# Weights of q and k loaded during the graph stage, and the last graph batch's tail spread over the engines

## The reference, cut to what matters

```python
# first layer: graph attention, two directions, 20 key rows, 16 heads
self_feat = concat([x, q_exp]) @ W_self.T + b_self
for d in range(2):
    w = softmax(where(mask, q @ k.T / sqrt(dh), NEG) + label_bias)
    output = output + (w @ kv) @ Wout[d] + bout[d]
x = x + relu(output)
# second layer
h = gamma * layernorm(x) + beta
q, k, v = split(h @ Wqkv.T + bqkv)                 # 16 heads of 32
att = softmax(q @ k.T) / sqrt(512)
h1 = (att @ v) @ Wp.T + bp + x
y = gamma * layernorm(h1) + beta + h1
```

## Time and profile before

| | |
|---|---|
| time, median of 3 runs | 1591.75 us (1589.45 to 1593.44) |
| the profiled execution | 1588.15 us, of which span 1586.4 |
| prologue | 0 to 116 us |
| graph stage | 116 to 652 us |
| attention stage | 652 us to the end |
| busy over the span | PE 87%, DVE 58%, POOL 57%, ACT 40% |
| mean granted TensorE clock | 0.927 of full speed |

### The profile page before, as it was taken

One profiled execution on the slowest core, in us unless ns is written; L12 is line 12 of the kernel. 1 busy time (PEld: TensorE's weight loads), 2 busy tenths in 40 slices (PEclk: granted clock), 3 DMA queues, 4 the chain that ended last, 5 costly groups with the idle time before them and its releaser, 6 DMA issues.

```text
span 1586.4 us, 19843 instructions
## 1 busy us (share of the span) xinstructions
PE 1376.4 (87%) x5988; PEld 873.2 (55%) x5988; DVE 923.2 (58%) x1494; ACT 631.1 (40%) x1090; POOL 899.5 (57%) x568
## 2 busy tenths in 40 slices
PE   6986998898898995279999999999999999999974
PEld 3644665665665663155565656555556555656532
DVE  2541665665664755136566757576667566666744
ACT  0231323324334232315454545545545445454551
POOL 1004434545545524316466958778769578687793
PEclk9997899999998987579999999999999999999977
DMA  9454213333323212724224425344344244253310
GB/s 297 177 174 129 83 65 132 136 113 135 125 106 153 86 60 106 265 73 109 73 61 127 114 61 147 94 107 108 87 127 111 62 127 111 70 143 89 104 46 27
DMA packets 107192, 179.41 MB, mean 113 GB/s; under 512 B 41312, under 2 KB 50848, under 8 KB 101840
## 3 DMA queue, kind: packets, MB, share of 16 engines
q1 hardware_dynamic: 94976, 143.92, 29.5%
q10 hardware_dynamic: 12112, 34.24, 7.2%
HBM read 81.06 MB, written 46.17 MB: 80 GB/s over the span
## 4 chain that ended last, share of the span: by engine, by line
PE 19%; POOL 17%; issue 8%; DVE 8%; ACT 3%; DMA 1%; SPq 1%; ACTq 1%; POOLq 0%; DVEq 0%
POOL acc L1022 7%; PE a_bank L1444 4%; PE a_bank L1407 4%; DVE rden L1295 4%; POOL acc L1017 3%; PE a_bank L1420 3%; PE a_bank L48 2%; PE a_bank L49 2%; PE a_bank L50 2%; DVE mx L1277 2%; PE a_bank L1455 2%; POOL h L1046 2%; POOL tn L1045 2%; ACT pt L1169 1%; DMA pt<-in_wp_t 1%
## 5 line engine op out<-in xcount | busy, mean ns | idle before, releaser
L1277 DVE TENSOR_REDUCE mx<-a_bank 128x1 f32<-128x512 f32 x512 | 341.9, 674 | 275.0 <-PE a_bank L1420 273.3
L1169 ACT ACTIVATE pt<-a_bank 128x512 f32<-128x512 f32 x512 | 301.9, 597 | 380.6 <-PE a_bank L1407 354.7
L1022 POOL TENSOR_TENSOR acc<-acc,pt 128x1024 f32<-128x1024 f32 x128 | 305.1, 2384 | 18.1 <-ACT pt L1169 9.9
L1407 PE MATMUL a_bank<-sq_stack,sk_stack 98*128 98x512 f32 x512 | 227.6, 447 | 31.1 <-ACT pt L1169 15.1
L1420 PE MATMUL a_bank<-sk_stack,sq_stack 96*128 96x512 f32 x512 | 220.0, 433 | 21.0 <-DVE mx L1277 19.7
L1017 POOL TENSOR_TENSOR acc<-pt 128x1024 f32<-128x1024 f32 x64 | 152.7, 2386 | 117.4 <-PE a_bank L1455 77.4
L1407 PEld LDWEIGHTS a_bank<-sq_stack,sk_stack 98*128 98x128 f32 x512 | 98.6, 193 | 158.3 <-issue 97.7
L774 PE MATMUL g_bank<-m,sf 128*128 128x320 f32 x512 | 161.9, 461 | 1.9 <-issue 1.9
L1420 PEld LDWEIGHTS a_bank<-sk_stack,sq_stack 96*128 96x128 f32 x512 | 99.9, 195 | 68.7 <-DVE mx L1277 54.6
L1295 DVE RECIPROCAL rden<-a_bank 128x128 f32<-128x128 f32 x128 | 120.1, 942 | 20.2 <-PE a_bank L1455 20.2
L48 PE MATMUL a_bank<-hh,wqkh 128*128 128x512 f32 x256 | 104.4, 408 | 27.5 <-DVE wqkl L1365 27.5
(11 more groups left out here) (164 smaller groups left out, 2540.6 us busy)
## 6 DMA issues: line engine op xcount, KB each, us to landing
sq_stack<-qh SPq DMA_DIRECT2D x256, 64.0 KB, 2.0
sk_stack<-kh SPq DMA_DIRECT2D x256, 64.0 KB, 2.3
m_rows<-mout SPq DMA_DIRECT2D x8, 1280.0 KB, 5.0
m<-m_rows SPq DMA_DIRECT2D x8, 1280.0 KB, 5.7
xraw<-in_x_t SPq DMA_DIRECT2D x8, 1024.0 KB, 7.5
xn<-in_x SPq DMA_DIRECT2D x8, 1024.0 KB, 6.8
h_rows<-xn ACTq DMA_DIRECT2D x8, 1024.0 KB, 3.9
t_rows<-houth SPq DMA_DIRECT2D x8, 1024.0 KB, 3.9
```

Of the source, the lines that this page charges most:

```text
L1022: nc.gpsimd.tensor_tensor(acc[:, two, :], acc[:, two, :], pt[:, step + 1, two, :], ALU.add).then_inc(s["sum_done"], 1)
L1169: nc.scalar.activation(pt[:, i, 2 * half + k, :], bank[:, k, :], ACT.Exp).then_inc(s["exp_done"], 1)
L1277: nc.vector.reduce_max(mx[:, half, k, n:n + 1], bank[:, 2 + e % 2, :], AX).then_inc(s["emax_done"], 1)
L1407: nc.tensor.matmul(bank[:, k, :], sk[0:3 * DH + 2, c % 2, j, i * P:(i + 1) * P], sq[0:3 * DH + 2, c % 2, j, :], start=True, stop=True).the ...
```

## The change

- The tile `v` and the four semaphores of the raw weights are made outside of the blocks, so that they exist through all of them. To make room, `vparts` of the prologue lies in the first half of `wself_raw`, and DVE waits for POOL's `w1l` before it writes there.
- SP loads the raw weights of q and k at the end of steps 1 and 2 of the graph stage into v[:, 0] and v[:, 1]. At the attention stage's start it loads v's and wp's only.
- The split into high and low parts is made by chunks of 512 columns, with a semaphore count for each. ACT's order is: q, k, qh of unit (0,0), v, kh, three values, wp. DVE's: q, k, ql, v, kl, ql and kl of unit (0,1). TensorE waits chunk by chunk.
- In the last graph batch DVE makes `hout` from PSUM, ACT rounds it into `houth`, POOL subtracts for chunks 0 and 2 and DVE for 1 and 3. DVE then adds bp to the four tiles of xn, behind everything else. ACT issues the h store after that.

```diff
--- before.py
+++ after.py
@@ -76,7 +76,7 @@
         mout = sb("mout", [P, 2, B, HK])
-        vparts = sb("vparts", [P, 2, 2, D], F32R)
+        vparts = wself_raw[:, 0:FC, :].rearrange("p (g k) o -> p g k o", g=2).bitcast(F32R)
         bank = ctx.enter_context(nc.psum_tensor("p_bank", [P, 8, 512], F32))
@@ -219,6 +219,8 @@
                     dve.wait_ge(s["v_ready"], n + 1)
+                    if n == 0:
+                        dve.wait_ge(s["w1_split"], 1)
                     if e == 1:
...
@@ -442,6 +444,9 @@
                     load_m(b + 1)
+                if isinstance(b, int) and b < 3:
+                    sp.dma_start(t["v"][:, b - 1], d["wqkv_t"][:, b - 1, :].rearrange("(c p) o -> p c o", p=P)
+                                 ).then_inc(t["w_in"][b - 1], 16)
@@ -537,9 +542,10 @@
             back(B - 1)
-            for i in range(NT):
-                add_bp(B - 1, i)
-            lo_rows(B - 1)
+            for f in (0, 2):
+                pool.wait_ge(s["lnt_done"], 4 * (B - 1) + f + 1)
+                nc.gpsimd.tensor_tensor(houtl[:, f, :], hout[:, f, :], houth[:, f, :].bitcast(F32),
+                                        ALU.subtract).then_inc(s["hl_done"], 1)
@@ -626,8 +632,10 @@
             normalise(B - 1)
+            act.wait_ge(s["t_stored"], 32 * (B - 1))
             for f in range(FC):
-                scale_ln(B - 1, f)
+                act.wait_ge(s["ho_done"], f + 1)
+                nc.scalar.activation(houth[:, f, :], hout[:, f, :], ACT.Copy).then_inc(s["lnt_done"], 1)
             store_h(B - 1)
@@ -734,6 +742,18 @@
             residual_ln(B - 1)
+            dve.wait_ge(s["gb_in"], 16 * 2 * FC)
+            dve.wait_ge(s["hl_done"], 4 * (B - 1))
+            for f in range(FC):
+                dve.wait_ge(s["lnt_ready"], 4 * (B - 1) + f + 1)
+                nc.vector.tensor_scalar(hout[:, f, :], bank[:, 2 + f, :], gcol[:, f, B - 1:B], bcol[:, f, B - 1:B],
+                                        ALU.mult, ALU.add).then_inc(s["ho_done"], 1)
+            for f in (1, 3):
+                dve.wait_ge(s["lnt_done"], 4 * (B - 1) + f + 1)
+                nc.vector.tensor_tensor(houtl[:, f, :], hout[:, f, :], houth[:, f, :].bitcast(F32),
+                                        ALU.subtract).then_inc(s["hl_done"], 1)
+            for i in range(NT):
+                nc.vector.tensor_tensor(xn[:, i, :], xn[:, i, :], bp[:, :], ALU.add).then_inc(s["hb_done"], 1)
@@ -865,7 +885,7 @@
         sq, sk = sb("sq_stack", [P, 2, HC, N], F32R), sb("sk_stack", [P, 2, HC, N], F32R)
-        v = sb("v", [P, 2, NT, D])
+        v = t["v"]
         pt = sb("pt", [P, NT, HC, N])
...
@@ -893,11 +913,11 @@
         STK = 16 * 6
-        w_in = tuple(s["w_in%d" % k] for k in range(4))
+        w_in = t["w_in"]
         t_in = (s["t_in0"], s["t_in1"])
...
-        raw = tuple(pt[:, k] for k in range(4))
+        raw = (v[:, 0], v[:, 1], pt[:, 0], pt[:, 1])
         hi_lo = ((t["wqkh"][:, :, 0:D], t["wqkl"][:, :, 0:D]), (t["wqkh"][:, :, D:2 * D], t["wqkl"][:, :, D:2 * D]),
@@ -989,7 +1009,7 @@
             sp.dma_start(bcol3[:, :, :], d["bqkc"]).then_inc(s["ld_c"], 16)
-            for k in range(4):
+            for k in (2, 3):
                 src = d["wqkv_t"][:, k, :] if k < 3 else d["wp_t"]
@@ -1006,6 +1026,13 @@
         def _(pool):
+            def split_lo():
+
+                for f in range(FC):
+                    pool.wait_ge(s["wp_hi"], f + 1)
+                    nc.gpsimd.tensor_tensor(hi_lo[3][1][:, f, :], raw[3][:, f, :], hi_lo[3][0][:, f, :].bitcast(F32),
+                                            ALU.subtract).then_inc(s["wp_lo"], 1)
+
             def key_sum(b, c, half, step):
@@ -1080,8 +1107,7 @@
             pool.wait_ge(s["set_up"], 3)
-            pool.wait_ge(s["w_hi"], 4)
-            nc.gpsimd.tensor_tensor(hi_lo[3][1], raw[3], hi_lo[3][0].bitcast(F32), ALU.subtract).then_inc(s["w_lo_pool"], 1)
+            split_lo()
             batches(pool, batch)
@@ -1097,6 +1123,13 @@
         def _(act):
+            def split_hi(k, chunks):
+
+                act.wait_ge(w_in[k], 16)
+                for f in chunks:
+                    nc.scalar.activation(hi_lo[k][0][:, f, :], raw[k][:, f, :], ACT.Copy
+                                         ).then_inc(s["w_hi"] if k < 3 else s["wp_hi"], 1)
+
             def load_t(b):
@@ -1239,13 +1272,14 @@
             act.wait_ge(s["ld_c"], 16)
-            for k in range(4):
-                act.wait_ge(w_in[k], 16)
-                nc.scalar.activation(hi_lo[k][0], raw[k], ACT.Copy).then_inc(s["w_hi"], 1)
+            split_hi(0, range(FC))
+            split_hi(1, range(FC))
             project(0, 0, 0)
+            split_hi(2, range(FC))
             project(0, 0, 1)
...
                 values(0, 0, i, src)
+            split_hi(3, range(FC))
             project(0, 1, 0)
@@ -1360,12 +1394,19 @@
             dve.wait_ge(s["bv_done"], 1)
-            for k in range(3):
-                dve.wait_ge(s["w_hi"], k + 1)
-                nc.vector.tensor_tensor(hi_lo[k][1], raw[k], hi_lo[k][0].bitcast(F32), ALU.subtract).then_inc(s["w_lo"], 1)
-            for c in range(2):
-                lo_part(0, c, 0)
-                lo_part(0, c, 1)
+            def split_lo(k):
+                for f in range(FC):
+                    dve.wait_ge(s["w_hi"], FC * k + f + 1)
+                    nc.vector.tensor_tensor(hi_lo[k][1][:, f, :], raw[k][:, f, :], hi_lo[k][0][:, f, :].bitcast(F32),
+                                            ALU.subtract).then_inc(s["w_lo"], 1)
+
+            split_lo(0)
+            split_lo(1)
+            lo_part(0, 0, 0)
+            split_lo(2)
+            lo_part(0, 0, 1)
+            lo_part(0, 1, 0)
+            lo_part(0, 1, 1)
             for slot in range(SLOTS):
@@ -1561,15 +1602,14 @@
-            pe.wait_ge(s["w_lo"], 1)
-            for f in range(FC):
-                project(0, 0, 0, f)
-            pe.wait_ge(s["w_lo"], 2)
-            for f in range(FC):
-                project(0, 0, 1, f)
-            pe.wait_ge(s["w_lo"], 3)
+            for which in range(2):
+                for f in range(FC):
+                    pe.wait_ge(s["w_lo"], FC * which + f + 1)
+                    project(0, 0, which, f)
             for i, dst in enumerate((OB, XB, 0)):
                 for f in range(FC):
+                    if i == 0:
+                        pe.wait_ge(s["w_lo"], FC * 2 + f + 1)
                     values(0, i, dst, f)
@@ -1582,7 +1622,7 @@
             shift_t(0, 0, 0)
-            pe.wait_ge(s["w_lo_pool"], 1)
+            pe.wait_ge(s["wp_lo"], FC)
             batches(pe, batch)
@@ -1601,6 +1641,8 @@
         t["ident"] = outer.enter_context(nc.sbuf_tensor("ident", [P, P], F32R))
+        t["v"] = outer.enter_context(nc.sbuf_tensor("v", [P, 2, NT, D], F32))
+        t["w_in"] = tuple(outer.enter_context(nc.semaphore("w_in%d" % k)) for k in range(4))
         with ExitStack() as ctx:
```

More of the change, by code:

```diff
@@ L376, in graph @@
                           "rc_done w_done wtr_ready wh_done wl_done att_mm att_done back_ready h_done "
-                          "st_done mv_done ve_done rstd_done ln_done lnt_ready lnt_done h_stored t_stored bp_in hb_done hl_done")
+                          "st_done mv_done ve_done rstd_done ln_done lnt_ready lnt_done h_stored t_stored bp_in hb_done hl_done ho_done")
         block = ctx.enter_context(nc.Block())
@@ L885, in attention @@
         OB, XB, QB, KB = 4, 5, 6, 7
-        s = sems(nc, ctx, "w_in0 w_in1 w_in2 w_in3 w_hi w_lo w_lo_pool ld_c t_in0 t_in1 h_in0 h_in1 h4_in rows_in "
+        s = sems(nc, ctx, "w_hi w_lo wp_hi wp_lo ld_c t_in0 t_in1 h_in0 h_in1 h4_in rows_in "
                           "stq00 stq01 stq10 stq11 stk00 stk01 stk10 stk11 set_up bv_done q_ready k_ready qh_done ql_done "
```

## The result

The changed kernel ran in 1581.67 us, median of four runs (1578.47 to 1584.23), against 1592.6 for the kernel before. The ratio is 0.9945, interval 0.9921 to 0.9968: 5 to 13 us faster. (The quotient of the two medians is 0.9931, inside that interval.) A second series gave 0.9942 (0.9919 to 0.9966); of its 23 runs of the kernel before, three took 1635 to 1934 us at a lower granted clock and are not in the ratio. The profiled execution took 1584.23, span 1582.4, against 1588.15 and 1586.4 before.

A forecast was written before the change was run, and what follows sets the result against it. The bound was the chain of waits from graph to attention stage, through raw weights and SP's 24 issues. Hand-over -8.3, covers and early loads 0, tail +1.3 gave -7.0 us: median 1584.8 from 1591.75, range 1580.5 to 1588.5.

The forecast's parts named there:

- The gain to kh of (0,1): Hand-over to attention: q and k loaded early and split by chunk let SP start at 667.6, not 675.9, gaining 8.3 us.
- The cost of the tail: Graph stage's last batch: arithmetic done 1.2 us sooner, but three stores in one piece end later, costing 1.3 us.
- My sum: Whole kernel: -8.3 for the hand-over, 0 for covers and early loads, +1.3 for the tail, together -7.0 us.
- rival (a): Hand-over: t lands up to 4 us earlier, so the gain is 10 and the time 1581.7; chance 0.10.
- The clock: TensorE at the attention start: the clock rises 4.4 us after the pause, at 668.3, so kh is just in time.
- rival (d): Attention start: TensorE's broken start keeps it at 1.2 GHz, slower at 1597, deciding from 53 low-clock matmuls; chance 0.04.
- Cover: TensorE ends k of (0,1) at 683.8, SP's last landing is 685.0: 1.2 us cover, cost 0 with 1 in range.
- DVE against POOL: Tail's subtractions: an exclusive lock makes them take turns, DVE's f = 3 ending at 644.2; without it the tail costs 0.3.
- Round-robin: Attention start's loads: DMA engines alternate between queues with work, so t lands as before; otherwise up to 4 us more gain.

The follow-up runs named there:

- weights alone: The changed kernel with the old tail of the last graph batch put back; ratio 0.9937 to the kernel before.
- tail alone: The kernel before with only the change's lines for the last graph batch on POOL, ACT and DVE; ratio 1.0009 to the kernel before.
- t loads first: The changed kernel, but SP issues v's and wp's raw weights only after the first half of hh and hl has landed; ratio 0.9926 to the kernel before.
- whole split: The changed kernel with each raw weight rounded and subtracted in one instruction instead of by chunk; ratio 0.9953 to the kernel before.
- maxima early: The early h store kernel, with unit (0,0)'s first eight maxima and their scores ahead of work for unit (0,1); ratio 0.9876 to the kernel before.
- all three: The maxima early kernel with SP's loads held back until the first half of t has landed; ratio 0.9871 to the kernel before.
- early h store: The changed kernel, but POOL adds bp ahead of its low parts and ACT issues the h store after its second rounding; ratio 0.9931 to the kernel before.

## Why the prediction was right

**Right, with sizes.** The raw weights leave the chain and hl's second half takes their place: TensorE started 7.48 us after the stage's start (7.5 forecast), stood still from 663.9 to 665.0, and SP's first stack came at 15.15 (15.4). The gain to kh of (0,1) is 41.10 - 32.90 = 8.2 (8.3). The cost of the tail is 1.19 (1.3), with the stores at 644.21 and 646.62 (644.2 and 646.6). Together 7.0 us, and 6.95 in the chain. The experiments separate both: weights alone 8.2 to 10.0, tail alone -1.24.

**The size of the whole.** 1584.8 was forecast, 1581.67 measured, that is 10.9 less by medians and 8.8 by the ratio instead of 7.0. No step of the sum is off by as much. Three things scatter: the start of the last `ln` (629.6 to 639.2 over ten traces, with the two kernels that lack the early loads in the middle, 634.1 and 634.3, so these loads cost the graph stage nothing that can be seen); the clock in the first 14 us of the attention stage, which was up before q had ended in four of the eight traces with early loads (weights only, t loads first, whole split, maxima early), worth 1.3 us where it rose before the second half; and the length from the first key sum to the end, 866 to 873. My sum was from one execution of each kind, and took a clock that stays low through q. It also had all later work hang rigidly on the chain; in one pair of traces the lead of 7.1 us at the first key sum was 4.1 at the 63rd, so a gain at the hand-over can be read at the hand-over, not from two spans. Whether the last 2 us are more than scatter stays open. The measured 1581.67 is just the number of rival (a), but its mechanism isn't in the trace: t did not land earlier (9.94 us from issue for hl's second half), except where SP was held back (t loads first and all three). That the median fell on that rival's number is luck.

**The clock.** I reckoned that it rises 4.4 us after TensorE's restart. In the changed kernel it nearly did (low until 669.6, restart at 665.0), in its second series it took 3.3. With the weights alone it was up at 664, before the restart, with no longer run of work behind it. So that step of the working was right by chance, on the careful side; rival (d), a clock kept low for 53 matmuls, occurred in no trace; the longest stretch that a pause gave in the hand-over was nine.

**Cover.** The 1.2 us of cover behind k of unit (0,1) held in the changed kernel: its last matmul began at 684.77 and SP's last landing was at 686.33. But the price of losing it, "0 to 1", was too low. With whole splits kh of (0,1) came 1.5 us later although q was not late; there the pause of 2.2 us was followed by a stretch at half speed that cost 1.6.

**DVE against POOL.** The forecast was that they take turns. In the changed kernel's rows above POOL's subtraction starts at 641.80 and lasts 1.83, DVE's two start at 641.83 and last 2.35. Alone they take 1.27 and twice 0.6; 1.27 + 1.2 = 2.47 one after the other, and 2.4 passed from 641.80 to 644.18. POOL's 1.83 is 0.6 more than alone, one DVE subtraction: DVE's first went ahead of it, and DVE's second came after. With the early h store, where the starts are again 0.03 apart, POOL went first and only DVE is longer:

```profile
642.28 1.26 POOL L549 TENSOR_TENSOR houtl<-hout,houth 128x512 fp32r<-128x512 f32 x1 [0.27 <-ACT houth L640]
642.31 2.38 DVE L756 TENSOR_TENSOR houtl<-hout,houth 128x512 fp32r<-128x512 f32 x2
```

The Trainium skill (SBUF — State Buffer, "SBUF: two separate sides") has it as an exclusive lock held for a whole instruction, and both pairs of rows agree. Who goes first isn't decided by the start that the trace shows: POOL's is the earlier one in both.

**Round-robin.** I took t's landings as unchanged when half of SP's weights were gone: 9.94 against 10.1. One trace of a kind scatters by more than that difference: with four weights on SP's queue hl's second half took 10.1 and 11.3 us, with two 9.9 to 11.4. When SP was held back it took 8.1 and 8.3, outside of both. The Trainium skill (DMA: Bandwidth & Descriptors, "Queues, rings and completion order") says that each DMA engine goes round-robin between the queues that have work. The runs agree with it: what counted was whether SP's queue had work while t was in flight, not how much it had in all.

## What to carry to other kernels

When loads are taken off a busy moment, ask which transfer lands last next, and whether the other queue is still full during it; the gain ends there. A store that is moved behind the others can lengthen the stage by its own transfer time even if the arithmetic ends sooner (2.4 us for the 1 MB of h here), so put stores out as their data is ready and give the later engine time to the rest. And look at what each engine's queue holds in front of critical work: the 7 us between the early h store and the early maxima (first key sum 55.40 against 48.68) were neither loads nor arithmetic saved, but work for the next unit that stood ahead of the scores on TensorE and of the maxima on DVE.

## What the runs showed that was not expected

A pause of TensorE of 2.2 us in the first stretch was followed by nine matmuls at half speed, 1.6 us more (whole split, above). In maxima early one of 1.75 us ahead of the first scores was followed by eight, in all three one of 1.25 at the same place by none. The pauses of 0.3 to 1.2 us between q's halves kept nothing down: in the four traces named above the clock rose during such a pause or within 1.3 us of its end. In the others it rose 3.3 to 5.5 us after it. What decides between the two isn't in these traces.

The last row of the chain above: the 4 KB shift row of unit (0,2) on ACT's queue took 8.02 us to land. A row of the same size for unit (0,0), on SP's queue and with no large transfer in flight, took 1.90. The slow one was issued at 741.59 behind 2 MB of t loads on the same queue (737.5 to 739.6). The other kernels whose chain shows it have 7.57 to 8.08. TensorE had other work for most of that time and waited 1.37 us for it:

```profile
742.58 0.80 PE L1461 MATMUL a_bank<-sk_stack,sq_stack 96*128 96x512 f32 x1 [1.11 <-DVE mx L1311]
...
750.53 0.47 PE L1448 MATMUL a_bank<-sq_stack,sk_stack 98*128 98x512 f32 x1 [1.37 <-DMA sq_stack<-sht]
```

The clock fell twice here:

```profile
744.00:746.00 2.00, 2.00 (x11) 0.62 (x13) 1.65 (x4) 1.03 (x2) 1.48 (x1) 0.50 1.05 305
...
748.00:750.00 2.00, 1.15 (x6) 0.30 (x2) 0.69 (x1) 0.60 (x1) 0.36 (x1) 0.95 0.38 92
...
752.00:754.00 2.00, 2.00 (x6) 1.33 (x5) 0.71 (x2) 0.60 (x1) 0.00 (x0) 0.50 0.27 65
```

It was at half speed from 742 to 748 and once more from 752 to 755. The first fall came while TensorE was waiting for DVE's maxima, before it waited for the row; the second 1.3 us after the wait for the row. In the kernel before it fell once at this place, and between these key sums the changed kernel gave back 2.5 of its 7.1 us. In its second series it gave back nothing there. Whether the row lands sooner when it doesn't stand behind the t loads, and what that would be worth, was not tried.
